# Cross-attention in two layers on one core: the part that makes queries joined with the part that makes keys and values, with transposed inputs laid out by the host

## What is computed

```
q = x @ w_q;  k, v = text @ w_k, text @ w_v            # 20 heads of 8
out_text = softmax(q k^T / sqrt(8)) v
k_ip, v_ip = ip @ w_k_ip, ip @ w_v_ip                   # 8 or 4 rows
layer 0: out_ip = softmax(q k_ip^T / sqrt(8) + box_mask) v_ip
layer 1: sem = l2norm(probs_text @ text) . l2norm(ip)
         out_ip = spatial * softmax(q k_ip^T / sqrt(8) + 0.5 sem) v_ip
x = x + (out_text + out_ip) @ w_out + b_out
```

## Time and profile before

| | us |
|---|---|
| median of 3 runs | 1537.2 (1537.09 to 1539.86) |
| the profiled run | 1539.36 |
| span of its profile | 1537.6 |
| `attend` begins (first score) | 203.9 |

### The profile page before, as it was taken

The page is one execution under the profiler, slowest core; times in us unless marked ns, Lnnn a source line. Parts: engine busy times, 40 slices in busy tenths (PEclk is TensorE's granted clock), DMA queues, the critical chain, the costliest instruction groups (busy, mean ns, idle before and its releaser), DMA issues. The chain is left out here.

```text
span 1537.6 us, 32818 instructions
## 1 busy us (share of the span) xinstructions
PE 1463.5 (95%) x12886; PEld 912.5 (59%) x12886; DVE 1122.0 (73%) x1602; ACT 1069.2 (70%) x1974; POOL 189.1 (12%) x363
## 2 busy tenths in 40 slices
PE   7888969999999999999999999999999999999998
PEld 4455523333333333477777777777777777777776
DVE  5777778887787877876767777777767777777742
ACT  2445548877877877876767778777777777787762
POOL 4563300000101101100001000000000000000000
PEclk9899869999999999899999999999999999999997
DMA  5156851111221211110010111000100011001000
GB/s 154 59 170 184 231 119 51 51 51 42 56 55 44 65 45 47 47 26 22 18 26 23 30 26 27 23 19 24 27 23 21 22 26 26 21 20 26 7 1 18
DMA packets 82839, 75.91 MB, mean 49 GB/s; under 512 B 28544, under 2 KB 70900, under 8 KB 82692
## 3 DMA queue, kind: packets, MB, share of 16 engines
q1 hardware_dynamic: 82692, 73.87, 18.1%
HBM read 47.73 MB, written 26.09 MB: 48 GB/s over the span
## 5 line engine op out<-in xcount | busy, mean ns | idle before, releaser
L1389 DVE TENSOR_TENSOR whole<-late,whole 128x1024 f16<-128x1024 f32 (+1 forms) x280 | 319.9, 1142 | 101.6 <-ACT whole L1243 98.4
L1129 PE MATMUL ps_v<-eh,whole 128*128 128x269 f16 x1040 | 292.5, 281 | 0.0
L1374 DVE TENSOR_REDUCE mx<-ps_y 128x2 f32<-128x800 f32 (+2 forms) x227 | 223.7, 986 | 93.3 <-PE ps_y L1051 92.9
L1129 PE MATMUL ps_n<-eh,whole 128*128 128x269 f16 x1040 | 291.4, 280 | 0.0
L1243 ACT CAST whole<-late 128x1024 f16<-128x1024 f32 (+1 forms) x280 | 275.6, 984 | 8.9
L1132 PE MATMUL ps_v<-eh,whole 128*128 128x269 f16 x960 | 268.7, 280 | 0.0
L1131 PE MATMUL ps_v<-el,whole 128*128 128x269 f16 x960 | 268.6, 280 | 0.0
L1132 PE MATMUL ps_n<-eh,whole 128*128 128x269 f16 x960 | 268.1, 279 | 0.0
L1131 PE MATMUL ps_n<-el,whole 128*128 128x269 f16 x960 | 267.9, 279 | 0.0
L1374 DVE TENSOR_REDUCE mx<-ps_x 128x2 f32<-128x800 f32 (+2 forms) x198 | 195.3, 986 | 79.2 <-PE ps_x L1051 79.0
L1374 DVE TENSOR_REDUCE mx<-ps_t 128x2 f32<-128x800 f32 (+2 forms) x215 | 211.3, 983 | 32.2 <-PE ps_t L1051 31.9
(11 more groups left out here) (435 smaller groups left out, 2093.1 us busy)
## 6 DMA issues: line engine op xcount, KB each, us to landing
e<-in_ctx SPq DMA_DIRECT2D x4, 1536.0 KB
kb<-k_parts SPq DMA_DIRECT2D x80, 74.9 KB
kb<-k_parts SPq DMA_DIRECT2D x80, 74.7 KB
k_parts<-kp SPq DMA_DIRECT2D x12, 400.0 KB
vb<-v_cols SPq DMA_DIRECT2D x40, 117.0 KB, 2.1
v_cols<-late SPq DMA_DIRECT2D x4, 1040.0 KB, 11.4
late<-v_cols SPq DMA_DIRECT2D x40, 104.0 KB, 2.0
qb<-q_parts SPq DMA_DIRECT2D x160, 25.0 KB
```

The costliest lines, as they stand in the source:

```text
L1129: pe.matmul(ps, hi, eh, start=(t == 0), stop=False)
L1374: nc.vector.tensor_reduce(mx[:, pair % 2, c, :], bank("max", pair, c)[:, :, 0:w], AX.X, ALU.max).then_inc(chunk_max, 1)
L1389: nc.vector.tensor_tensor(pl[s % 2][:, t0:t0 + w, :], ring[:, turn % EXPS, 0:w], ph[s % 2][:, t0:t0 + w, :], ALU.subtract).then_inc(low_do ...
```

## The change

- `queries` and `prepare` become one block: `queries` now returns a program for each engine, which `prepare` calls first. The scores of the small attention free their banks one by one (`sc_out`) for the key groups of batch 0.
- The host gives `c_xT`, `c_ctxT` (context transposed), `c_tokT` (the last rows transposed) and `c_ctx` (context padded to 13 tiles, each partition's rows side by side). The transposes on PE, their copies, and the token loads go. The context of the next batch is one DMA; its transposed form comes in four pieces of 400 columns, 0.41 MB each (`load_piece`), a piece when PE has read the old columns for the last time.
- The maximum over partitions: DVE multiplies the identity by the column of maxima, PE multiplies it by ones into the free columns 400 to 511 of two key banks (112 columns and 16), DVE reduces each and joins the two.
- The second key part moves from DVE to ACT, one group behind the first part. The scale bits come after group 3 instead of 1, ACT's scaling after group 5 instead of 3, DVE's f16 remainders after groups 7 and 8 instead of 5 and 6.
- Key sends are waited for in three parts (`k_sent[m]`) instead of as a whole.
- SP's order in a batch: keys of segment 0; next context; keys of segment 1; four transposed pieces; keys of segment 2; values (layer 0 in one DMA instead of two); from batch 2 on one `load_pair`. Pairs 2 and 3 are loaded at the start of `attend`.
- The next batch's context maximum is taken by DVE after value tile 9. `centre` stands at the end of batch 0, `normalise` at the end of batch 1. Batches are written out, without a loop.
- The rows of ones in `kb` come by DMA (`c_kb1`) instead of POOL memsets.

```diff
-                    sp.dma_start(e32[:, 0:NT - 1, :], src[0:P * (NT - 1)].rearrange("(t p) c -> p t c", p=P)).then_inc(ctx_loaded, 16)
-                    sp.dma_start(e32[0:LAST, NT - 1, :], src[P * (NT - 1):TOK]).then_inc(ctx_loaded, 16)
...
+                def load_turned(b, kc):
+                    n = LASTF if kc == 3 else KI + ((kc + 1) * KC - 1) // P
+                    sp.wait_ge(filled[n % 8], fills(b - 1, n))
+                    load_piece(sp, consts, ctxT, turned_in, b, kc)
+
+                first["sync"](sp)
+                for b in range(B):
+                    send_keys(b, 0)
+                    if b < B - 1:
+                        sp.wait_ge(el_done, 2 * (b + 1))
+                        sp.dma_start(e32[:], consts["ctx"][b + 1]).then_inc(ctx_loaded, 16)
+                    send_keys(b, 1)
+                    if b < B - 1:
+                        for kc in range(4):
+                            load_turned(b + 1, kc)
+                    send_keys(b, 2)
+                    if b < B - 1:
+                        sp.wait_ge(freed[LASTF % 8], fills(b, LASTF))
+                        send_v0(sp, K, VS, vaug, b)
+                        send_cut_v(sp, K, VS, L, b)
+                    if b >= 2:
...
+                        load_pair(sp, K, KS, QS, b - 2)
...
+                def turn_maximum(ps, which, part, count):
+                    c0, c1 = MAX_IN[part]
+                    pe.wait_ge(spread_done, count)
+                    return pe.matmul(ps[:, KC:KC + c1 - c0], ones[:], spread[which][:, c0:c1], start=True, stop=True)
...
+                            pe.wait_ge(turned_in[kc], 16 * (b + 1))
...
-                        last.then_inc(filled[(TR + n) % 8], 1)
+                        if not b and n < 2:
+                            last = turn_maximum(ps, 1, n, 1)
+                        elif n in (2, 3):
+                            last = turn_maximum(ps, 0, n - 2, b + 2)
+                        last.then_inc(filled[n % 8], 1)
...
+                def second_part(b, n):
+                    m, kc = n // 4, n % 4
+                    act.wait_ge(freed[n % 8], fills(b, n))
+                    nc.scalar.copy(kp[:, m, 1, kc * KC:(kc + 1) * KC], rem[:, (KI * b + n) % RR, :]).then_inc(k1_done, 1)
...
+                        if kc == 0 and b:
+                            act.wait_ge(k_sent[m], 16 * SENDS[m] * b)
+                        act.wait_ge(filled[n % 8], fills(b, n))
+                        nc.scalar.copy(kp[:, m, 0, kc * KC:(kc + 1) * KC], banks[n % 8][:, 0:KC]).then_inc(k0_done, 1)
+                        if n:
+                            second_part(b, n - 1)
+                        if n == 5:
+                            high(b)
...
-                    nc.gpsimd.partition_all_reduce(amax[:, 1:2], amax[:, 0:1], P, bass.bass_isa.ReduceOp.max).then_inc(amax_all, 1)
...
+                def spread_out(m, count):
+                    dve.wait_ge(amax_done, count)
+                    nc.vector.tensor_scalar(spread[m][:], K["ident"][:], amax[:, 2 * m:2 * m + 1], None, ALU.mult).then_inc(spread_done, 1)
...
+                def over_partitions(n, part):
+                    c0, c1 = MAX_IN[part]
+                    nc.vector.tensor_reduce(share[:, part:part + 1], banks[n][:, KC:KC + c1 - c0], AX.X, ALU.max).then_inc(amax_all, 1)
...
-                        nc.vector.tensor_copy(k1, r).then_inc(k1_done, 1)
...
+                        if n == 3:
+                            scale_bits(b)
+                        if n in (7, 8):
+                            low(b, n - 7)
...
+                        if t == 9 and b < B - 1:
+                            largest(b + 1)
+                    if b == 0:
+                        centre(nc.vector, link, L, 0, L["mask"], smax).then_inc(centred, 1)
...
+    sp.dma_start(ctxT[:, :, k0:k1], consts["ctxT"][b, :, k0:k1].rearrange("(c p) k -> p c k", p=P)).then_inc(turned_in[kc], 16)
...
             def _(sp):
-                vaug, vcut = LS[0]["vaug"], LS[0]["vcut"]
...
+                load_pair(sp, K, KS, QS, 2)
+                send_v0(sp, K, VS, vaug, B - 1)
                 send_cut_v(sp, K, VS, LS[0], B - 1)
+                load_pair(sp, K, KS, QS, 3)
```

More of the change, by code:

```diff
@@ L27 @@
 U32 = mybir.dt.uint32
+U16 = mybir.dt.uint16
 ALU = mybir.AluOpType
@@ L287, in sem @@
             return st.enter_context(nc.semaphore(name))
[L289 to L294, removed]
+        e32, ctxT, ctx_loaded, turned_in = ctx
+        wk, wv, weights_in = w_ctx
+        ones = first["ones"]
+        KI, KC = 10, 400
+        SENDS = (3, 6, 6)
         kp = sbuf("kp", [P, 3, 3, NK], BF16)
@@ L352, in send @@
[L352 to L366, removed]
@@ L405, in batch @@
+                first["tensor"](pe)
+                pe.wait_ge(weights_in, 64)
+                for b in range(B):
                     for n in range(KI):
@@ L407, in batch @@
                         if m == 0:
[L408 to L411 removed]
+                            pe.wait_ge(turned_in[kc], 16 * (b + 1))
+                        ps = bank(b, n)
                         for c in range(2):
@@ new lines, in _ @@
+                first["scalar"](act)
+                for b in range(B):
+                    for n in range(KI):
+                        m, kc = n // 4, n % 4
+                        if kc == 0 and b:
[6 more added lines that the diff above has]
+                            high(b)
+                    second_part(b, KI - 1)
+                    if b == 1:
@@ new lines, in low @@
+                def low(b, piece):
+                    t0, t1, rows = ((0, NT - 1, P), (NT - 1, NT, TXT[1] - P * (NT - 1)))[piece]
+                    dve.wait_ge(eh_done, 2 * b + piece + 1)
+                    part = K["eh"][LOW:LOW + rows] if t0 else K["el"][0:rows]
+                    nc.vector.scalar_tensor_tensor(out=part[:, b, t0:t1, AT:AT + C], in0=e32[0:rows, t0:t1, :],
+                                                   scalar=scales[0:rows, 0:1].bitcast(F32),
+                                                   in1=K["eh"][0:rows, b, t0:t1, AT:AT + C], op0=ALU.mult, op1=ALU.subtract).then_inc(el_done, 1)
@@ L615, in batch @@
-                    if first:
-                        dve.wait_ge(exp_done, 1)
-                        link(normalise(nc.vector, link, L, 0, None, ssum))
+                        if not b and n < 2:
+                            over_partitions(n, n)
+                        elif n in (2, 3):
+                            over_partitions(n, n - 2)
+                        nc.vector.tensor_tensor(rem[:, (KI * b + n) % RR, :], banks[n % 8][:, 0:KC], kp[:, m, 0, kc * KC:(kc + 1) * KC],
+                                                ALU.subtract).then_inc(freed[n % 8], 1)
```

853 lines of the change are left out of this document (399 added, 454 removed).

## The result

The changed kernel takes 1523.42 us (median of 4 runs, 1523.06 to 1523.84) beside 1538.33 for the kernel before (four runs; the table above has three of them): ratio 0.9905, 95% interval 0.9889 to 0.9921. It is faster by 14.9 us, clear of the spread; 29.3 were forecast.

What follows compares the result with a forecast made beforehand. TensorE was taken as busy for 1463.5 of 1537.6 us, nearly all in the unchanged loop; query part, batches and 2 for clock start the loop at 174.6 instead of 203.9: 1537.2 - 29.3 = 1507.9, said 1508, range 1497 to 1525.

Steps and rivals of the forecast that it cites:

- What bounds a batch start: Starts of batches 1 to 3: TensorE waits for the DMA of the transposed context, near 66, 102 and 136 us.
- The next context: From context buffer release to transposed piece 0 landing: 3.31 MB at 350 GB/s plus 1.8, 11.3 us; bounds 9.6 and 21.9.
- Query part: Head before batch 0's key projections: 5.7 + 11.0 + 8.9 + 4.7 = 30.3 us, 14.9 earlier than 45.24.
- VectorE's lag: Batch 0: first remainder 3.6 to 7.0 us after TensorE's start, 6.5 taken, with masks and maxima in front.
- A batch from its first remainder: Within a batch, from VectorE's first remainder until the context buffer is free: 18.2 us.
- Second parts to ScalarE: Key casts in each batch: ten more on ScalarE, 4.5 us per batch, and VectorE loses as much.
- Maxima by TensorE: Per batch, multiplies and small reductions, some 1.5 us on VectorE, replace GpSimd's all-reduce with 7.5 us behind it.
- The last batch: Batch 3, no context to fetch: VectorE ends near 32, SP's sends last, 36.3 us in all, to 172.6.
- Serial pieces: Rival at the transposed pieces: each takes 3.3 us after the one before, 5.9 a batch; 1526; chance 0.14 with similar losses.
- Pieces so late that the kernel is slower: Rival at batch starts: at 165 GB/s piece 0 lands 21.9 us after the release; 1550, chance 0.06.
- handed back: Rival: the loop's opening, VectorE's lag through batch 3 or GpSimd's blocks return the whole gain; 1537, chance 0.05.
- TensorE as the bound: Rival in the batches: piece 0 lands within 8 us of the release, batches take 130 instead of 142.3; 1496, chance 0.13.

Runs made afterwards that it cites:

- even split: Changed kernel with both layers' key arrays joined, so segment 1's keys go out as three sends of 128 rows instead of six: 1515.63 us.
- the combined one: Changed kernel with joined key array and three sends of 128 rows, transposed pieces 0 to 2 before them, GpSimd's fills and bias add moved: 1506.43 us.

## Why the prediction was right or wrong

Forecast and measured dates of TensorE, and the release of each context buffer:

```
                    forecast   measured
keys of batch 0       30.3       32.16
release in batch 0    55.0       57.7
batch 1               66.3       72.42
batch 2              101.8      110.45
batch 3              136.3      149.94
loop                 174.6      187.47
```

*What bounds a batch start* was right: TensorE waits for the DMA of the transposed pieces and for nothing else, three times. The loop behind it was carried over rightly (1334.2 for 1333.7).

*The next context* was the step that failed. The forecast put 3.31 MB at one rate, 350 GB/s, between rows of other mixes, 11.3 in all; measured 14.7 to 14.8, three times 3.5, 10.4 of the missing 12.9. The volume was right and so was the order. What was wrong was to price the queue as one pipe: 16 engines work off their own shares, and the six key sends give four of them twice the mean and another four nothing. The keys then end 6.0 us behind the context instead of 2.9. With an even split, the term measured 12.4 and 11.6 in batches 2 and 3, close to what was forecast, but still 14.5 in batch 1, where the cause is open. The code could have said it: the key sends' shape stands there, 4 and 12 heads, and the bound of 21.9 was drawn from a different cause. The rate was also misread: of the two stretches taken for context and keys together only the one of 422 GB/s had both; in that of 361 only rows of 1024 B moved, the context's.

*Query part*: 1.9 late. From the first projection to the value tables 12.2 for 11.0, of it 0.68 for `bias`, which I had called no bound; from there to the scores 9.6 for 8.9, with VectorE's cuts slowed by GpSimd's fills (three casts took 0.82, 1.35 and 2.77, with the fills moved 0.69, 0.67 and 0.68); the scores themselves 4.4 for 4.7.

*VectorE's lag*: the first remainder comes 8.2 behind TensorE's start, beyond the bounds of 3.6 to 7.0; 6.5 were taken. VectorE's timeline (L529 the context maximum, L596 the first remainder, L567 the end of the context's scaling):

```profile
34.77 3.61 DVE L529 TENSOR_REDUCE amax<-e 128x1 f32<-128x3328 f32 x1
...
40.32 0.57 DVE L596 TENSOR_TENSOR res<-ps_x,kp 128x400 f32<-128x400 f32 x1
...
57.13 0.56 DVE L567 SCALAR_TENSOR_TENSOR eh<-e,scales,eh 61x256 f16<-61x256 f32 x1
```

The masks ran to 33.9, 1.8 behind TensorE's start, and stood in front of both maxima and of 1.9 us of memsets and small steps. *A batch from its first remainder* took 17.4 (57.7 - 40.3) for 18.2, so the release is only 0.8 late against the batch's start. In batches 1 and 2 the release came 23.2 and 24.7 behind the start for 24.2 and 23.2.

*Second parts to ScalarE* were counted as 4.5 us a batch off VectorE; undone, they change nothing that is clear of the spread. *Maxima by TensorE* were worth 6.3, in batch 0 alone. *The last batch* took 37.5 for 36.3: SyncE was last, as said, and its sends are slow for the reason above (32.8 with the even split).

*The rivals.* Serial pieces gave 1526, near the measured time, but did not happen: TensorE waits for piece 0 alone. That 1523.42 lies inside the stated 1497 to 1525 is luck: the upper end was put there for this rival. Pieces so late that the kernel is slower, at 195 GB/s, did not happen; the mean up to piece 0 was 3.31 MB in 14.8 - 1.8 = 13 us, 255 GB/s (an estimate), between that and the 350. Nothing was handed back in the loop. TensorE as the bound, 1496, was reached by no kernel; the combined one, 1506.43, comes nearest, with VectorE still in its way.

## What to carry to other kernels

Price a queue of transfers by its fullest engine, not by bytes over one rate: write down for each transfer how many engines it ran on here (4, 8, 12 or 16, by its heads), add up the rows on each, and see which transfer stands behind the fullest. A load that TensorE waits for belongs in front of stores nobody waits for, but not in front of a load that others wait for sooner, if it has to wait itself. And look at where GpSimd's long fills lie against VectorE's casts before trusting a time that a fraction of a microsecond can turn.

## What the runs showed of the hardware

- Three sends of 32 rows and 4 heads with three of 96 and 12 close with 48 writes, three of 128 rows with 48 as well: 4 for a send of 4 heads, 8 for one of 8, 16 for one of 16. At equal bytes the last row of the even split leaves 3.1 us sooner (2.9 against 6.0 behind the context's last).
- A cast of 128x1024 on VectorE took 0.70, or 6.20 to 6.73 us where it began 0.43 to 0.96 us behind the start of GpSimd's copies with fills right behind these; with the fills moved it took 0.69, begun 0.76 behind. The Trainium skill, SBUF — State Buffer, section Who interferes with whom, says that the order of issue decides who blocks; the rows agree, and here the cast waited through three fills in a row, not one instruction.
- After a wait of 5.5 to 6.7 us at a batch start TensorE's granted clock was 0.50, that is 1.2 GHz, and two key groups took 4.4 to 5.7 us instead of 2.9. With three sends they took 4.40 behind a wait of 3.10 (granted clock 0.50) and 2.95 behind one of 3.46 (1.00): the length of the wait alone does not decide.
